# Cross-attention and routed FFN on one core: softmax probabilities held in three buffers, transposed two steps after their scores, and GpSimd's inverse root placed ahead of a step's masks

## What is computed

```python
x   = x + attention(layernorm(x), ctx, ctx)    # x, ctx: (128, 64, 128); 16 heads of width 8
x   = x + moe(layernorm(x))                    # 8 experts, D=128, F=512, one expert per token

# attention, per sequence of 64 tokens and per head
scores = einsum('bhqd,bhkd->bhqk', q, k) / sqrt(8)
out    = einsum('bhqk,bhkd->bhqd', softmax(scores), v)   # then @ Wo.T + bo

# moe, over the 8192 tokens
expert = argmax(xf @ Wr.T + br)
y      = relu(xf @ W1[expert].T + b1[expert]) @ W2[expert].T + b2[expert]
```

## Time and profile before

| what | value |
| --- | --- |
| median of 3 runs | 562.91 us (560.3 to 563.98) |
| the profiled execution | 563.26 us, its span 561.3 us |
| granted TensorE clock, mean over the span | 0.939 |
| first scores to last scores of the second stage (start to start) | 71.07 to 349.67 us |
| scores of tile 4 to scores of tile 63 | 259.95 us for 59 steps, 4.41 us each |

### The profile page before, as it was taken

How to read it: one execution, slowest core, us unless ns; L and a number is a source line. 1 busy time by engine, 2 the same in 40 slices (tenths; PEclk the granted TensorE clock), 3 DMA queues, 4 the chain that set the end, 5 groups by cost and what they waited for, 6 DMA issues and landing times.

```text
span 561.3 us, 19186 instructions
## 1 busy us (share of the span) xinstructions
PE 472.0 (84%) x6467; PEld 356.3 (63%) x6468; DVE 408.6 (73%) x1053; ACT 310.0 (55%) x584; POOL 235.0 (42%) x391
## 2 busy tenths in 40 slices
PE   1999968899989899898998989760099999999992
PEld 1666634566656566565665656650099999999991
DVE  6789555687978789787987878543457777778771
ACT  1677745565655555555565654300067777777770
POOL 6233212212226437255273562735524444454442
PEclk9999979999999999999999998955579999999997
DMA  7355100000011101111021110920212222222220
GB/s 248 114 151 149 40 19 18 17 18 18 17 20 45 27 22 49 21 35 36 14 58 22 33 30 1 356 76 24 87 50 68 65 69 65 65 65 66 66 60 0
DMA packets 32480, 33.74 MB, mean 60 GB/s; under 512 B 6419, under 2 KB 25750, under 8 KB 32160
## 3 DMA queue, kind: packets, MB, share of 16 engines
q1 hardware_dynamic: 28096, 24.33, 16.3%
q0 software_dynamic: 4320, 8.53, 4.5%
HBM read 19.10 MB, written 9.99 MB: 52 GB/s over the span
## 4 chain that ended last, share of the span: by engine, by line
PE 56%; DVE 15%; issue 13%; POOL 7%; ACT 5%; DMA 2%; SPq 1%; DVEq 0%; POOLq 0%
PE PS L918 12%; PE PS L931 11%; PE PS L796 7%; PE PS L809 5%; DVE SB L635 4%; DVE MX L627 4%; ACT SB L494 4%; PE PS L780 3%; PE PS L879 3%; PE PS L785 3%; POOL rows L425 3%; PE PS L767 3%; PE PS L888 3%; PE PS L904 1%; PE PS L844 1%
## 5 line engine op out<-in xcount | busy, mean ns | idle before, releaser
L403 POOL TENSOR_TENSOR VP<-BIG,C 128x128 f32<-128x128 f32 x128 | 56.1, 460 | 155.7 <-PE PS L888 152.8
L796 PEld LDWEIGHTS PS<-C,SB 128*128 128x128 f32 x512 | 55.2, 143 | 80.8 <-ACT SB L494 66.9
L627 DVE TENSOR_REDUCE MX<-PS 128x16 f32<-128x1024 f32 x64 | 78.2, 1222 | 38.3 <-PE PS L809 37.2
L435 POOL DMA_INDIRECT out<-SB,BIG x71 | 69.0, 972 | 82.3 <-DVE SB L751 79.2
L796 PE MATMUL PS<-C,SB 128*128 128x128 f32 x512 | 85.4, 290 | 18.4 <-ACT SB L494 12.7
L510 ACT COPY KM<-BIG 128x644 f32 x71 | 51.8, 729 | 55.0 <-PE PS L918 29.2
L494 ACT ACTIVATE SB<-SB 128x1024 f32<-128x1024 f32 x64 | 67.7, 1058 | 23.5 <-DVE SB L635 23.0
L918 PE MATMUL PS<-BIG,KM 128*128 128x128 f32 x568 | 79.8, 282 | 0.4
L635 DVE TENSOR_TENSOR SB<-PS,MX 128x1024 f32<-128x1024 f32 x64 | 77.4, 1209 | 1.7
L931 PE MATMUL PS<-KM,SB 128*128 x568 | 76.0, 277 | 0.6 <-ACT SB L514 0.6
L918 PEld LDWEIGHTS PS<-BIG,KM 128*128 128x128 f32 x568 | 71.8, 195 | 3.0 <-issue 1.7
(11 more groups left out here) (108 smaller groups left out, 690.8 us busy)
## 6 DMA issues: line engine op xcount, KB each, us to landing
BIG<-rows SPq DMA_DIRECT2D x71, 66.0 KB
X<-in_x SPq DMA_DIRECT2D x16, 256.0 KB, 3.2
PT<-in_ctxT SPq DMA_DIRECT2D x16, 256.0 KB, 2.8
KM<-BIG SPq DMA_DIRECT2D x256, 16.0 KB
BIG<-in_we SPq DMA_DIRECT2D x1, 2576.0 KB, 12.7
KM<-in_w SPq DMA_DIRECT2D x1, 2048.0 KB, 9.0
out<-SB,BIG POOLq DMA_INDIRECT x71
rows<-X,DESTI POOLq DMA_INDIRECT x64, 2.4
```

Of the source, the lines that this page charges most:

```text
L403: last = nc.gpsimd.tensor_tensor(dst, v, own, ALU.mult)
L435: nc.gpsimd.indirect_dma_start(out=out, out_offset=bass.IndirectOffsetOnAxis(ap=RT[:, s.r, ID:ID + 1].bitcast(i32), axis=0), in_=YO[:, s.r ...
L627: nc.vector.tensor_reduce(MX[:, n % 2, :], sc, axis=AX.X, op=ALU.max).then_inc(mx_done, 1)
L796: last = nc.tensor.transpose(bank(4)[:, i * P:(i + 1) * P], SB[:, n % 2, hp * P:(hp + 1) * P], ident)
```

## The change

The buffer SB gets a third part, used by n modulo 3. TensorE transposes tile n-2 in place of n-1 in step n, and does the products with V for n-3 in place of n-2. All that follows (RD, NUM, L651, L654, statistics, routing) moves one step later with it; there is one step more in all. ScalarE's copies in step n are then those of tile n-2, its exponential still that of tile n. GpSimd's masks of tile t move from step t to step t+1 (which still waits for the same products as before), and the Newton iteration stands ahead of the masks of its step in place of behind them and behind the start of the scatter.

```diff
-L_RD = 6
-L_MUL = 7
-L_X1 = 8
+L_RD = 7
+L_MUL = 8
+L_X1 = 9
...
-M_SEED = 17
-M_INV = (18, 19)
+M_SEED = 18
+M_INV = (19, 20)
...
-M_TOP = 20
+M_TOP = 21
...
-        SB = sb("SB", P, 2, H * SEQ)
+        SB = sb("SB", P, 3, H * SEQ)
...
             def masks(s):
-                if s.n < NT:
-                    t = s
-                    need(pool, od_done, t.n - 1)
+                j = s.batch(M_INV[0])
+                if j is not None:
+                    pool.wait_ge(seed_step, 4 * j + 4)
+                    newton(j, 0, 6)
+                j = s.batch(M_INV[1])
+                if j is not None:
+                    newton(j, 6, INV_STEPS)
+                t = s.n - 1
+                if 0 <= t < NT:
+                    need(pool, od_done, t - 1)
...
             def softmax(s):
-                if 1 <= n < NT + 1:
-                    act.wait_ge(pt_done, 2 * (n - 1) + 1)
-                    nc.scalar.copy(PT[:, (n - 1) % 2, 0:4, :].rearrange("p a b -> p (a b)"), bank(4)).then_inc(pt_ready, 1)
+                if 2 <= n < NT + 2:
+                    act.wait_ge(pt_done, 2 * (n - 2) + 1)
+                    nc.scalar.copy(PT[:, n % 2, 0:4, :].rearrange("p a b -> p (a b)"), bank(4)).then_inc(pt_ready, 1)
...
-                    nc.scalar.activation(SB[:, n % 2, :], SB[:, n % 2, :], ACT.Exp, scale=SCALE).then_inc(exp_done, 1)
+                    nc.scalar.activation(SB[:, n % 3, :], SB[:, n % 3, :], ACT.Exp, scale=SCALE).then_inc(exp_done, 1)
...
-                    need(dve, pt_done, 2 * (n - 1))
+                    need(dve, pt_done, 2 * (n - 2))
...
             def stage2(s):
-                m = n - 1
+                m = n - 2
                 if 0 <= m < NT:
                     pe.wait_ge(exp_done, m + 1)
                     need(pe, pt_ready, 2 * m)
...
-                m = n - 2
+                m = n - 3
                 if 0 <= m < NT:
                     pe.wait_ge(pt_ready, 2 * m + 2)
                     pe.wait_ge(vp_done, m + 1)
```

More of the change, by code:

```diff
@@ L76, in constants @@
     return c, pad, ids
-L_RD = 6
-L_MUL = 7
-L_X1 = 8
+L_RD = 7
+L_MUL = 8
+L_X1 = 9
 M_BN = L_X1 + 1
 M_MOM = M_BN + ST - 1
-M_SEED = 17
-M_INV = (18, 19)
+M_SEED = 18
+M_INV = (19, 20)
 M_TR = L_X1 + 2
 M_LG = M_TR + 1
-M_TOP = 20
[L91 to L94, removed]
+M_TOP = 21
+M_HOT = 22
+M_RANK = 22
+M_POS = 23
+M_OUT = 23
 INV_STEPS = 12
@@ L394, in masks @@
             def masks(s):
-                if s.n < NT:
-                    t = s
-                    need(pool, od_done, t.n - 1)
+                j = s.batch(M_INV[0])
[8 more added lines that the diff above has]
+                    need(pool, od_done, t - 1)
                     for z in range(2):
-                        dst = VP[:, t.r % 2].rearrange("p b (c z) m -> p (b c) z m", z=2)[:, :, z, 16 * z:16 * z + 16].rearrange("p g (r w) -> p g r w", w=DK)
-                        v = V[:, bass.ds(t.n * P, P)].rearrange("p (g z w) -> p g z w", z=2, w=DK)[:, :, z, :].unsqueeze(2).to_broadcast([P, 8, 2, DK])
+                        dst = VP[:, t % 2].rearrange("p b (c z) m -> p (b c) z m", z=2)[:, :, z, 16 * z:16 * z + 16].rearrange("p g (r w) -> p g r w", w=DK)
+                        v = V[:, bass.ds(t * P, P)].rearrange("p (g z w) -> p g z w", z=2, w=DK)[:, :, z, :].unsqueeze(2).to_broadcast([P, 8, 2, DK])
                         own = C[:, C_OWN:C_OWN + 2 * DK].rearrange("p (r w) -> p r w", w=DK).unsqueeze(1).to_broadcast([P, 8, 2, DK])
@@ L413, in masks @@
                     pool.sem_inc(sent, 1)
[L414 to L420, removed]
                 for t in range(ST):
@@ L475, in softmax @@
                 n = s.n
[L476 to L479, removed]
-                if 1 <= n < NT + 1:
-                    act.wait_ge(pt_done, 2 * (n - 1) + 1)
-                    nc.scalar.copy(PT[:, (n - 1) % 2, 0:4, :].rearrange("p a b -> p (a b)"), bank(4)).then_inc(pt_ready, 1)
+                if 4 <= n < NT + 4:
+                    act.wait_ge(od_done, n - 3)
+                    need(act, ot_ready, n - 11)
+                    nc.scalar.copy(NUM[:, (n - 4) % 8, :], bank(6)[:, P * (n % 2):P * (n % 2) + P]).then_inc(num_kept, 1)
+                if 2 <= n < NT + 2:
+                    act.wait_ge(pt_done, 2 * (n - 2) + 1)
+                    nc.scalar.copy(PT[:, n % 2, 0:4, :].rearrange("p a b -> p (a b)"), bank(4)).then_inc(pt_ready, 1)
                 for i in range(4):
@@ L488, in softmax @@
                         nc.scalar.copy(X1T[:, i].rearrange("p t d -> p (t d)"), bank(6)[:, 2 * P:4 * P]).then_inc(x1t_ready, 1)
-                if 1 <= n < NT + 1:
-                    act.wait_ge(pt_done, 2 * (n - 1) + 2)
-                    nc.scalar.copy(PT[:, (n - 1) % 2, 4:8, :].rearrange("p a b -> p (a b)"), bank(4)).then_inc(pt_ready, 1)
+                if 2 <= n < NT + 2:
+                    act.wait_ge(pt_done, 2 * (n - 2) + 2)
+                    nc.scalar.copy(PT[:, n % 2, 4:8, :].rearrange("p a b -> p (a b)"), bank(4)).then_inc(pt_ready, 1)
                 if n < NT:
                     act.wait_ge(sub_done, n + 1)
-                    nc.scalar.activation(SB[:, n % 2, :], SB[:, n % 2, :], ACT.Exp, scale=SCALE).then_inc(exp_done, 1)
+                    nc.scalar.activation(SB[:, n % 3, :], SB[:, n % 3, :], ACT.Exp, scale=SCALE).then_inc(exp_done, 1)
             each_step(softmax)
@@ L633, in stage2 @@
                     dve.wait_ge(mx_done, n + 1)
-                    need(dve, pt_done, 2 * (n - 1))
-                    nc.vector.tensor_tensor(SB[:, n % 2].rearrange("p (h k) -> p h k", h=H), sc,
+                    need(dve, pt_done, 2 * (n - 2))
+                    nc.vector.tensor_tensor(SB[:, n % 3].rearrange("p (h k) -> p h k", h=H), sc,
                                             MX[:, n % 2, :].unsqueeze(2).to_broadcast([P, H, SEQ]), ALU.subtract).then_inc(sub_done, 1)
@@ L795, in transposes @@
                     hp = 4 * half + i
-                    last = nc.tensor.transpose(bank(4)[:, i * P:(i + 1) * P], SB[:, n % 2, hp * P:(hp + 1) * P], ident)
+                    last = nc.tensor.transpose(bank(4)[:, i * P:(i + 1) * P], SB[:, n % 3, hp * P:(hp + 1) * P], ident)
                 last.then_inc(pt_done, 1)
@@ L859, in stage2 @@
                     if j is not None:
-                        need(pe, num_kept, min(n - 2, NT))
+                        need(pe, num_kept, min(n - 3, NT))
                         for t in range(2):
```

## The result

| | before | after |
| --- | --- | --- |
| median | 561.62 us (4 runs, 560.3 to 563.98) | 536.75 us (4 runs, 535.38 to 537.51) |
| ratio | | 0.955, 95% interval 0.9507 to 0.9593 |
| the profiled execution, its span | 563.26, 561.3 us | 536.78, 534.9 us |

The changed kernel is 25 us faster. The forecast was 541, its range 534 to 548.

A forecast was written before the change was run, and what follows sets the result against it. TensorE's work was taken to set 3.96 us a step, with waits adding 0.45 to a mean step. 59 steps (233.6) plus extras (4.5) from 89.7 end at 327.8, 21.9 us earlier than 349.67: 541 us, range 534 to 548.

The forecast's parts named there:

- TensorE's 3.96: In the loop, TensorE's own work sets 3.96 us a step; 59 steps take 233.6 us without extras.
- The exponential: Its wait ahead of TensorE's transposes, 0.4 to 0.5 us every fourth step, goes with transposes two steps behind.
- The lateness of VectorE: In the loop, VectorE is late locally: 0.4 + 0.1 + 0.1 us per eight steps, bounds 0 and 1.9.
- GpSimd's inverse root: In the loop, PREF stops waiting for GpSimd's Newton iteration; steps of 5.79 and 4.70 us fall to 3.96 and 4.15.
- The other signs: Profile after: steps of 4.3 at 3 modulo 8, 4.15 at 6; VectorE busy 37.5 of 40 us; last scores about 324.
- Start of the loop: Tile 5's scores after start at 89.7 us, as tile 4's before; bounds 1.0 us later, 2.0 earlier.
- The end: After the last scores, GpSimd's chain stays tied to the same step's end and runs as before.
- The experts' stage: The stage behind the loop, claimed to be untouched by the change.
- (a): Rival: VectorE or ScalarE sets the loop's pace, lateness carried on; cycle up to 34, 545 to 549 us; chance 0.17.
- (b): Rival: PREF's wait goes, the exponential's returns as a copy wait; 9.3 of 21.9 us lost, 550; chance 0.05.
- (c): Rival: TensorE has room below 3.96, VectorE's 30.4 a cycle sets pace; 527, milder forms 530 to 536; chance 0.10.
- (d): Rival: ScalarE's exponential closes a new loop; at 2.0 us longer, steps take 4.55, total 571 us; chance 0.02.

The follow-up runs named there:

- half products: The changed kernel with half of the products of probabilities and values left out (8 of the 16 matmuls of a tile): 528.4 us, ratio 0.9416.
- the first experiment: The kernel before with GpSimd's Newton iteration ahead of the masks of its step, transposes still one step behind: 547.17 us, ratio 0.9768.
- the repetition: The kernel before, unedited, profiled once more: 561.36 us, ratio 1.0005.

## Why the prediction was right

**TensorE's 3.96 is the floor, and the waits go.** Right. In 59 steps it takes 236.6 us, forecast 238.1. The half products show that the floor is work. The rule of the Trainium skill that was weighed against it (Perfetto Trace Analysis, Identifying the Most-Contended Engine) would have left TensorE a third of its time, since PEld is busy 26.75 of 40 us after; here the measurement decides for matmul busy time, 39.87 of 40, as less work for TensorE alone shortened seven steps of eight. The eighth is the one that waits for VectorE's reciprocal. In the rule's other half, that VectorE deserves the look, it isn't wrong: it is the next bound, 1 us a cycle away.

**The exponential.** Right: its wait is gone from the matmuls, and so is nearly all of the second payment behind PREF. The transposes alone give 2.4%. The small waits of TensorE for the copy L482 that were forecast in its place are not among the matmuls' waits; what was left came out at L888 instead.

**The lateness of VectorE, 0.6 us a cycle.** Right in mechanism, too large in size. In the profile after, step 35 reads:

```profile
210.03 1.22 DVE L627 TENSOR_REDUCE MX<-PS 128x16 f32<-128x1024 f32 x1
...
211.17 0.94 DVE L631 RECIPROCAL RD<-PS 128x128 f32<-128x128 f32 x1
...
212.16 0.38 PEld L888 LDWEIGHTS PS<-PT,C 128*32 128x32 f32 x16 [0.24 <-DVE RD L631]
```

The maxima start 1.54 us after the scores (208.49), 0.39 late, where 0.46 was measured in the earlier trace rows and taken over; the step pays 0.29 of it, and step 7 modulo 8 pays nothing, where 0.1 and another 0.1 for unequal steps were added. Measured 0.3 in place of 0.6, within the bounds of 0 to 1.9 that were given; over the loop the sum was 1.5 us too high.

**GpSimd's inverse root.** Right. The last Newton operation ends at 216.15, 3.4 us into the step that starts at 212.74; the forecast was 3.3. PREF starts at 216.89, when VectorE is free. But the reason could be put more simply, as the first experiment shows: the move ahead of the masks is enough by itself, without the later transposes.

**The other signs.** Steps of 4.3 at 3 modulo 8 and 4.15 at 6 modulo 8 came as forecast (4.25 and 4.15). VectorE was busy 36.95 of 40 us, forecast 37.5, and the last scores came at 321.46, forecast 324. None of the three signs of being wrong came: the maxima don't drift, L888 waits once in eight steps and not in every fourth, and the end didn't grow.

**Start of the loop.** I put the scores of tile 5 at 89.7; they came at 88.8. Of the 0.9, 0.3 are older than the loop, and the rest lies within the bounds given (2.0 earlier if the clock stays up: it does in some executions and with added matmuls, for 1.4 to 1.8). That the time of before could be set in for the time of after was in part luck: two profiles of before differ by 1.2 us here.

**The end.** Right that it moves unchanged with the last scores: 56.6 and 56.2 us to the experts. **The experts' stage** was taken as untouched and took 1.8 us less. That is the largest single part of the miss of 4.6 us in the profiled execution (541.4 against 536.8): 1.8, 1.5 for the lateness, 0.9 for the start, 0.4 for the end. Its cause isn't settled: it lies in the first three blocks and goes with the clock's rise there, and it goes with the place of the transposes in eleven profiles of twelve, but no run shows by what path.

**The rivals.** (a) needed lateness carried through the cycle. In the profile after, the maxima start 1.56 and 1.54 us after the scores in steps 34 and 35 and 1.15 to 1.21 in the other six; with 3.2 us more for VectorE they start 1.3 to 1.9 after them in all eight. (b) would have shown waits for the copy in every reciprocal step; there are none in the changed kernel, and 0.2 once a cycle when the reciprocal stands ahead. (c): no step of the changed kernel is under 3.95 us though nothing is waited for, and the half products show that TensorE's work makes it. (d): the path through ScalarE exists and costs 0.3 when the reciprocal no longer hides it, far from what (d) needed.

## What to carry to other kernels

Read the distance from start to start of a repeated instruction: the shortest step of a periodic loop is a good guess at its floor (an experiment that takes work away can confirm it, as here), and the sum of what the other steps are above it is the most that removing waits can give, here 259.95 - 59 x 3.96 = 26.3 us, of which 23.3 came. A wait costs more than its own entry when what it delays is due in the next step; slack of one more buffer takes away that second payment, and a better order on the releasing engine's queue takes away the wait and with it both. Where a helper engine serves two chains, ask at the end of the loop as well what stands ahead in its queue.

## What was not expected of the hardware

The granted clock at the start of the loop varies between executions of the same code in that place. With a wait of 1.81 us for the first subtraction and later ones for the copies it fell to 0.50 in the profiles that took 17.6 to 18.0 us to tile 5, and stayed at 1.00 in one with 16.22. Behind its start, and up to the last scores, it fell in one place only: where the last PREF within the loop was waited for. This is the kernel before, in which step 60 starts its L833 after 1.94 us of idling,

```profile
336.00:342.00 6.00, 4.30 (x66) 2.94 (x66) 4.42 (x12) 2.52 (x5) 1.60 (x6) 0.73 0.00 0
```

and that step takes 6.94 us (7.08 in the repetition), 1.1 to 1.3 more than the same step of the batches ahead of it; so about 1 of the 23.3 us that the change gained in the loop lies in this one step. The kernel with the transposes alone has the same dip (0.83 and 0.89 in two windows from 324 to 336 us); the changed kernel and the one with the order on GpSimd alone, in which PREF isn't waited for there, have none. Why the waits of 1.6 us in the earlier batches leave the clock alone isn't explained by these runs.
